# A graph network with routed experts on one core: four one-hot and message buffers in the value pass, the identity stored into the adjacency matrix beside the node MLP, and the last experts padded to 128 hidden units

## What is computed

```python
# layer 2, twice: softmax over the edges of a node, then its messages
msg = v[src] * alpha[:, :, None]
agg = jax.ops.segment_sum(msg, dst, num_segments=n).reshape(n, H * DV)
out = agg @ Wo
...
return jax.nn.relu(h @ w1 + b1) @ w2 + b2            # node MLP, 256 -> 1024 -> 256
# layer 3, three times: the neighbours' sum plus the node itself
pooled = jax.ops.segment_sum(msgs, row, num_segments=N_NODES) + h
hid = jax.nn.relu(_bn_train(pooled @ W1[l] + b1[l], g1[l], be1[l]))
# last experts: one of 32 per node, 256 -> 64 -> 256
h = jax.nn.relu(jnp.einsum('nd,ndh->nh', xf, w1t) + jnp.take(b1, idx, axis=0))
out = jnp.einsum('nh,nhd->nd', h, w2t) + jnp.take(b2, idx, axis=0)
```

## Time and profile before

| what | value |
|---|---|
| median of 3 runs | 6715.59 us (6714.32 to 6717.77) |
| the profiled execution: time, span of its instructions | 6709.0 us, 6707.0 us |
| mean granted clock of PE | 0.879 |
| PE busy | 5085.1 us, 76% |
| DVE, POOL, ACT busy | 2851.2, 2285.1, 1151.6 us |
| DMA | 949.50 MB, 142 GB/s on average |

### The profile page before, as it was taken

How to read it: one execution, slowest core, us unless ns; L and a number is a source line. 1 busy time by engine, 2 the same in 40 slices (tenths; PEclk the granted TensorE clock), 3 DMA queues, 4 the chain that set the end, 5 groups by cost and what they waited for, 6 DMA issues and landing times. The chain is left out here.

```text
span 6707.0 us, 87548 instructions
## 1 busy us (share of the span) xinstructions
PE 5085.1 (76%) x21976; PEld 3340.3 (50%) x21977; DVE 2851.2 (43%) x6134; ACT 1151.6 (17%) x2799; POOL 2285.1 (34%) x2415
## 2 busy tenths in 40 slices
PE   5657598979589795776496767496977997979857
PEld 3434475458435693443364433365876443434443
DVE  5575695041410424556685566685233102020242
ACT  2311251012100231111002111002322101010020
POOL 2786203704264050677230677230023000000014
PEclk9999999969789697889798888798978998989955
DMA  0000133427443262899572899571145332414134
GB/s 15 2 2 21 66 137 145 154 88 213 146 158 102 88 211 98 274 306 305 155 237 71 267 308 307 154 237 58 35 139 187 141 116 96 145 66 149 62 86 120
DMA packets 477264, 949.50 MB, mean 142 GB/s; under 512 B 111984, under 2 KB 285403, under 8 KB 474653
## 3 DMA queue, kind: packets, MB, share of 16 engines
q1 hardware_dynamic: 325308, 638.92, 28.2%
q0 software_dynamic: 114208, 281.05, 14.0%
q10 hardware_dynamic: 37568, 27.34, 1.4%
HBM read 732.28 MB, written 214.82 MB: 141 GB/s over the span
## 5 line engine op out<-in xcount | busy, mean ns | idle before, releaser
L1148 PE MATMUL banks<-ring,xn 128*128 128x512 f32 (+1 forms) x3500 | 1359.2, 551 | 144.4 <-DMA ring<-adjacency 144.4
L1148 PEld LDWEIGHTS banks<-ring,xn 128*128 128x128 f32 x3500 | 629.2, 192 | 862.5 <-issue 716.1
L991 POOL DMA_INDIRECT rows<-pairs,idxr x832 | 810.0, 974 | 239.3 <-issue 215.2
L1873 PE MATMUL banks<-agg,hotT 128*128 x1664 | 638.2, 488 | 235.3 <-issue 224.9
L1727 POOL IOTA found_i<- 128x25 int32 x4 | 0.6, 148 | 1808.1 <-ACTq L1723 1388.5
L381 POOL DMA_INDIRECT dst_table<-nodes_pay,nodes_row x392 | 378.8, 966 | 643.6 <-DVEq L1116 474.6
L1873 PEld LDWEIGHTS banks<-agg,hotT 128*128 128x128 f32 x1664 | 301.5, 223 | 522.6 <-issue 516.6
L381 POOL DMA_INDIRECT bin_table<-bins_pay,bins_row x392 | 457.9, 1168 | 270.2 <-DVE bins_row L767 119.1
L2126 PE MATMUL banks<-msg,hot 128*128 128x264 f32 x1664 | 429.0, 402 | 51.2 <-issue 24.9
L1846 DVE TENSOR_TENSOR prod<-banks,rows 128x512 f32<-128x512 f32 x416 | 267.9, 686 | 424.0 <-DMA rows<-pairs,idxr 311.6
L1056 PE MATMUL banks<-spans,lanes 128*128 128x256 f32 x1440 | 331.4, 387 | 119.5 <-DVE spans L1037 108.1
(11 more groups left out here) (350 smaller groups left out, 6798.6 us busy)
## 6 DMA issues: line engine op xcount, KB each, us to landing
ring<-adjacency SPq DMA_DIRECT2D x150, 1280.0 KB
spill<-rows SPq DMA_DIRECT2D x208, 512.0 KB
rows<-spill SPq DMA_DIRECT2D x208, 512.0 KB
w1r<-in_L_ffn_W SPq DMA_DIRECT2D x114, 512.0 KB
adjacency<-strips SPq DMA_DIRECT2D x13, 3200.0 KB
w1r<-in_L_ffn_w SPq DMA_DIRECT2D x65, 512.0 KB
rows<-home_rows SPq DMA_DIRECT2D x35, 640.0 KB
ring<-adjacency SPq DMA_DIRECT2D x25, 640.0 KB
```

What stands on the lines that cost most here:

```text
L991: nc.gpsimd.indirect_dma_start(rows[:, row, :], None, table, bass.IndirectOffsetOnAxis(ap=idxr[:, at + g:at + g + 1], axis=0))\
L1148: last = nc.tensor.matmul(K.ps[2 * (g % 2) + o][:, 0:wd], x[:, t * D + o * P:t * D + (o + 1) * P], ring[:, n % R, 0:wd // cols, q * SPAN_S ...
L1873: last = nc.tensor.matmul(K.ps[2 + 2 * (jj % 2) + g // 2][:, g % 2 * D:(g % 2 + 1) * D], hotT[:, jj % 2, g * P:(g + 1) * P], tile_of(q, t) ...
```

## The change

Three edits, independent of each other.

1. In `attention_values`, `hot` and `msg` have four buffers each, and DVE and POOL wait for PE's step i - 4. PE's program is the same but for the buffer that it reads.
2. `spmm` has no `own` any more. In `node_mlp`, SP loads the 25 diagonal squares (128x128) of the stored adjacency matrix, POOL adds the identity to them in one instruction, and SP writes them back and waits for that, so that the matrix that layer 3 reads holds the nodes themselves.
3. The last experts are padded with zeros to 128 hidden units: `b1T`, `w1r` and `hT` have 128 rows or columns, DVE clears `b1T` and `w1r` at the stage's start, and POOL clears the lower half of the second weights in the stage of the routing logits. All four expert stages have a new semaphore, `cleared`, for which SP waits ahead of its first fetch and ACT ahead of its bias loads; where the units are 512, DVE raises it at once.

```diff
@@ spmm
                                     ring[:, n % R, 0:wd // cols, q * SPAN_S:q * SPAN_S + cols],
-                                    start=(t == 0), stop=(t == NT - 1 and not own))
+                                    start=(t == 0), stop=(t == NT - 1))
                         last.then_inc(used, 1)
-                    if own:
-                        for q in range(wd // P):
-                            t = 4 * g + q
-                            for o in range(KD):
-                                last = nc.tensor.matmul(K.ps[2 * (g % 2) + o][:, q * P:(q + 1) * P],
-                                                        x[:, t * D + o * P:t * D + (o + 1) * P], K.ident[:, :],
-                                                        start=False, stop=(q == wd // P - 1))
-                        last.then_inc(summed, 1)
...
@@ class Second
+    def clear(self):
+        if self.hm < P:
+            self.nc.gpsimd.memset(self.second[self.hm:P, :], 0.0)
...
@@ routed_ffn
-        w1r = st.sb("w1r", [P, R, KD, hid])
+        w1r = st.sb("w1r", [P, R, KD, wide])
...
             def _(sp):
+                sp.wait_ge(cleared, 1)
...
-                                last = nc.tensor.matmul(K.ps[2 + jj % 2][0:hm, h * P:(h + 1) * P],
-                                                        w1r[:, jj, s, h * hm:(h + 1) * hm],
+                                last = nc.tensor.matmul(K.ps[2 + jj % 2][:, h * P:(h + 1) * P],
+                                                        w1r[:, jj, s, h * P:(h + 1) * P],
...
+                if hm < P:
+                    nc.vector.memset(b1T[:, :], 0.0)
+                    nc.vector.memset(w1r[:, :, :, :], 0.0).then_inc(cleared, 1)
+                else:
+                    dve.sem_inc(cleared, 1)
...
@@ attention_values
-        hot = st.sb("hot", [P, 2, GS, P])
-        msg = st.sb("msg", [P, 2, GS, W])
+        hot = st.sb("hot", [P, 4, GS, P])
+        msg = st.sb("msg", [P, 4, GS, W])
...
-                    wait_count(dve, summed, GS * (i - 1) + 1 if not isinstance(i, int) or i >= 2 else 0)
-                    one_hot(nc, edges, K, hot[:, j % 2, :, :], i)
+                    wait_count(dve, summed, GS * (i - 3) + 1 if not isinstance(i, int) or i >= 4 else 0)
+                    one_hot(nc, edges, K, hot[:, j, :, :], i)
...
@@ node_mlp
+    def diagonal(t):
+        at = t * SPAN_S + t % 2 * P
+        return K.adjacency[t // 2, :, at:at + P]
...
+                for t in range(NT):
+                    sp.dma_start(squares[:, t, :], diagonal(t)).then_inc(fetched, 16)
+                sp.wait_ge(raised, 1)
+                for t in range(NT):
+                    sp.dma_start(diagonal(t), squares[:, t, :]).then_inc(kept, 16)
+                sp.wait_ge(kept, 16 * NT)
+
+            @block.gpsimd
+            def _(pool):
+                pool.wait_ge(fetched, 16 * NT)
+                nc.gpsimd.tensor_tensor(squares[:, :, :], squares[:, :, :],
+                                        K.ident[:, :].unsqueeze(1).broadcast_to([P, NT, P]), ALU.add).then_inc(raised, 1)
```

More of the change, by code:

```diff
@@ L1096, in _, with spmm @@
                     sp.wait_ge(stored[h], 16 * ((NS + 1 - h) // 2))
-def spmm(nc, K, x, out, own=False, beside=None):
+def spmm(nc, K, x, out, beside=None):
     R, SLICE = 5, 5
@@ L1110, in spmm @@
         loaded = [st.sem(f"loaded{j}") for j in range(R)]
-        used, summed, kept = (st.sem(x) for x in ("used", "summed", "kept"))
+        used, kept = st.sem("used"), st.sem("kept")
         def width(g):
@@ L1164, in _ @@
                 for g in range(GROUPS):
-                    if own:
-                        act.wait_ge(summed, g + 1)
-                    else:
-                        act.wait_ge(used, (g + 1) * slices)
+                    act.wait_ge(used, (g + 1) * slices)
                     for o in range(KD):
@@ L1287, in dense @@
         with nc.Block() as block:
+            @block.gpsimd
+            def _(pool):
+                if ahead:
+                    ahead.clear()
             @block.sync
@@ L1518, in __init__ @@
         self.hm = min(P, self.hid)
-        self.second = st.sb("second", [self.hm, self.experts * (self.hid // self.hm) * D])
+        self.nc, self.second = st.nc, st.sb("second", [P, self.experts * (self.hid // self.hm) * D])
         self.w2 = w2
         self.whole = st.sem("whole")
+    def clear(self):
+        if self.hm < P:
+            self.nc.gpsimd.memset(self.second[self.hm:P, :], 0.0)
     def fetch(self, act):
-        act.dma_start(self.second[:, :].rearrange("p (n d) -> p n d", d=D),
+        act.dma_start(self.second[0:self.hm, :].rearrange("p (n d) -> p n d", d=D),
                       self.w2.rearrange("e (c p) d -> p (e c) d", p=self.hm)).then_inc(self.whole, 16)
@@ L1533, in routed_ffn @@
     nh = hid // hm
+    wide = nh * P
     n = r.chunks
@@ L1537, in routed_ffn @@
     with stage(nc) as st:
-        b1T = st.sb("b1T", [hm, experts * nh])
-        w1r = st.sb("w1r", [P, R, KD, hid])
+        b1T = st.sb("b1T", [P, experts * nh])
+        w1r = st.sb("w1r", [P, R, KD, wide])
         bias2 = st.sb("bias2", [P, experts * D])
@@ L1542, in routed_ffn @@
         xT = st.sb("xT", [P, 2, D])
-        hT = st.sb("hT", [hm, 2, nh * P])
+        hT = st.sb("hT", [P, 2, nh * P])
         yr = st.sb("yr", [P, R, D])
@@ L1547, in routed_ffn @@
         stored = [st.sem(f"stored{j}") for j in range(R)]
-        spread = st.sem("spread")
+        spread, cleared = st.sem("spread"), st.sem("cleared")
         biased, turned, copied, hidden, acted, summed, written = (
@@ L1621, in _ @@
             def _(act):
-                act.dma_start(b1T[:, :], b1.rearrange("e (c p) -> p (e c)", p=hm)).then_inc(biased, 16)
+                act.wait_ge(cleared, 1)
+                act.dma_start(b1T[0:hm, :], b1.rearrange("e (c p) -> p (e c)", p=hm)).then_inc(biased, 16)
                 act.dma_start(bias2[:, :], b2.rearrange("e d -> (e d)").partition_broadcast(P)).then_inc(spread, 16)
@@ L2106, in step @@
                 def step(i, j, k):
-                    wait_count(pool, summed, GS * (i - 1) + 1 if not isinstance(i, int) or i >= 2 else 0)
-                    nc.gpsimd.tensor_copy(msg[:, j % 2, :, D:W], weights[:, bass.ds(i * (GS * HEADS), GS * HEADS)]
+                    wait_count(pool, summed, GS * (i - 3) + 1 if not isinstance(i, int) or i >= 4 else 0)
+                    nc.gpsimd.tensor_copy(msg[:, j, :, D:W], weights[:, bass.ds(i * (GS * HEADS), GS * HEADS)]
                                           .rearrange("p (c h) -> p c h", h=HEADS)).then_inc(placed, 1)
@@ L2125, in step @@
                         pe.wait_ge(evacuated, v & 31)
-                        nc.tensor.matmul(K.banks[:, bass.ds((v % BANKS) * 512, W)], hot[:, j % 2, g, :], msg[:, j % 2, g, :],
+                        nc.tensor.matmul(K.banks[:, bass.ds((v % BANKS) * 512, W)], hot[:, j, g, :], msg[:, j, g, :],
                                          start=False, stop=True, skip_group_check=True).then_inc(summed, 1)
@@ L2158, in node_mlp @@
         hT = st.sb("hT", [P, 2, hid])
+        squares = st.sb("squares", [P, NT, P])
+        fetched, raised, kept = st.sem("fetched"), st.sem("raised"), st.sem("kept")
         loaded, staged, biased, turned, copied, hidden, acted, summed, added = (
@@ L2458, in layer3_gnn @@
         for l in range(layers):
-            spmm(nc, K, K.xn, K.agg, own=True)
+            spmm(nc, K, K.xn, K.agg)
             feature_layer(nc, K, K.agg, False, A["L3_gnn_W1"][l], A["L3_gnn_b1"][l], yT, S)
```

6 lines of the change are left out of this document (3 added, 3 removed).

## The result

| what | before | after |
|---|---|---|
| median of the runs | 6715.12 us, 4 runs (6714.32 to 6717.77) | 6588.71 us, 4 runs (6587.49 to 6590.15) |
| ratio | | 0.9817, interval 0.9805 to 0.9829 |
| the profiled execution: time, span | 6709.0, 6707.0 us | 6588.37, 6586.3 us |
| PE busy | 5085.1 us | 4944.6 us |

The account below looks back on a forecast made before the run. Bounds by stretch: PE-DVE hand-over in the value passes, PE in layer 3's products, PE with tile-shape changes in the last experts. Terms -66 - 34 - 13 + 1.5 = -111.5 from 6709.0 give 6597.5, plus 6.6: 6604 us, range 6580 to 6645.

Parts of the forecast that it names:

- a step of 1.87 us: Value passes: with four buffers the step falls from 2.20 to 1.87 us, 66 us less over two passes.
- near the upper end, because of the marks: Value passes: 1.87 us chosen between 1.78 and 1.92, because PE's four marks a step are not in its matmul rate.
- The 1.92 of the earlier trace: Upper bound of the value step, from the stage building the adjacency matrix: same PE program, 1.92 us a step, DVE 99% busy.
- some 60: Node MLP: the chain of loads, POOL's addition and stores lasts some 60 us at most, far inside the stage's 180.
- The 1 us at the start: Last experts' start: DVE's clearing of 1056 elements takes 0.9 us ahead of weight and bias loads, 1 us more.
- The 0.5 us for the semaphore: Three other expert stages: the new semaphore costs 0.1 to 0.2 us each, 0.5 us more.
- The offset to the median: Whole kernel: the median of the runs lies 6.6 us above the profiled execution, so 6597.5 becomes 6604 us.
- POOL's copy too late: Value passes: DVE, almost without gaps, keeps POOL's copy waiting; 6622 to 6670 us, chance 0.18.
- Padding brings nothing: Last experts: the 0.6 us between groups may come from PE reading the expert's number and stay; 6617 us, chance 0.17.
- Slower: Node MLP: the squares' chain of loads, add and stores outlasts the stage; 6744 us if it lasted 320, chance 0.03.
- the ring: Value passes: PE's and DVE's work and two hand-overs, 4.44 us, over two buffers 2.22 a step, over four 1.11.

Follow-up runs that it names:

- value_only: The kernel before with only the changed `attention_values` (four buffers of one-hots and messages): 7657.24 us, ratio 0.9893.
- own_left_out: The kernel before without layer 3's 50 matmuls against the identity and with nothing in their place: 7693.42 us, ratio 0.9932.
- half_before: The kernel before with the scatters of every second chunk of the last experts left out: 7780.31 us, ratio 0.9977, last experts 183.0 us.
- unroll12: The changed kernel with twelve steps instead of four in the value pass's loop body: 7678.84 us, ratio 0.9856.
- half_after: The changed kernel with the scatters of every second chunk of the last experts left out: 7651.24 us, ratio 0.9819, last experts 165.9 us.
- unroll12_again: The changed kernel with twelve steps in the value pass's loop body, run once more: passes 198.7 and 196.0 us.

## Why the prediction was right, and where its size was off

**Edit 1: the step fell as argued, its term was 7 us too small.** The prediction took a step of 1.87 us between bounds of 1.78 and 1.92 and said 66; measured was 1.84 and 73.1 (80 on the other chips). The bound of 1.78 was the step that runs, three times in four; "near the upper end, because of the marks" was the failed choice. The marks are read in every step and cost nothing in a step of 1.78. What lengthens a step by 0.28 comes once in a body of four and is gone with a body of twelve. The 1.92 of the earlier trace rows was a bound set by DVE and said nothing of PE. The other chips' passes are 6.6 us shorter in sum: the passes of the first chip have one wait of 2.5 us for POOL and 45 steps longer than 1.9 us, those of value_only no such wait and 32.

**Edit 2: right in all its terms.** 34.5 for 34 us in the products; cost in the node MLP +0.4 for 0 (0 to 3), with a chain of 35 us for "some 60" at most; the start delayed by 0.3 (PE's first record 9.27 us after SP's first load, 8.95 before). own_left_out shows, by its stages, that nothing of the saving is lost.

**Edit 3: right on the first chip, and only there.** 14.5 for 12 us: POOL's period in steady state is 2.57 where I had 2.55, PE takes no part, and PE's own chunk at the low clock is 2.13 us where I had 2.19. The term holds only while each chunk's sum is there when POOL comes to scatter it, a condition that the prediction did not name. On the other chips the padding gave 2 to 3 us in one trace and nothing in the next. That the limit before was PE at 2.80, and not POOL, was argued; half_before shows that 2.80 is PE's own pace. The 1 us at the start was about right: DVE's clearing of `w1r` takes 0.91 us, and PE's first record of the second product is 21.3 us after the stage's start where it was 19.8 (its very first records, transposes, came sooner, 3.9 us for 5.6). The 0.5 us for the semaphore in the three other expert stages does not show: they differ by +0.2, -0.3 and 0.0. POOL's clearing of the second weights takes 6.92 us under the routing logits, where the stage did not grow.

**The offset to the median** is 6 of the 15 us by which the forecast was high. I took the profiled execution of before to be 6.6 us below the median because it was, and added the 6.6 after; the changed kernel's profiled execution stands 0.3 below its own median. The rest is edit 1's 7 and edit 3's 2.5, less 1 or so in the other stages. The prediction's own range of 6583 to 6616 does not come out of its terms; edit 1's bounds and 4 us of edit 2 give 6586 to 6618. The measured 6588.71 lies in both.

**The rivals.** POOL's copy too late: real, 2.5 us once, at the first pass's start, and nowhere in the steady state. Its price was set for a copy locked out in every step. Steady copies last 0.755 us with DVE 97% busy, and so they do in unroll12 with DVE 100% busy. The difference seen in the rows is that in the steady state both instructions start together, while at the start DVE has buffers free and waits for nothing. That alone is not the cause: every pass with four buffers starts so, and the copy was through in 0.81 or 0.93 us in eight of twelve. What decides stays open. The Trainium skill (SBUF — State Buffer, "SBUF: two separate sides") has the shared port taken for a whole instruction by whoever is first. The steady 0.755 agrees with a copy that gets in at an instruction's end; the 7.77 us does not, it outlasts eight of DVE's instructions. The measurement decides: the copy can be passed over again and again.

Padding brings nothing: not so on the first chip; PE's own chunk became shorter, 2.13 for 2.81 us at the same clock, and half_before and half_after agree, with 372 and 410 records in the same time. Slower: nothing of it, the chain takes 35 of 195 us.

## What to carry to other kernels

When two engines wait for each other's buffers in turn, add the four parts of the ring (both works, both hand-overs), divide by the number of buffers, and compare with each engine alone; once buffers have made the ring harmless, look at each engine's own step, and next at a cost that comes once in a loop body. Read a stage that seems to be at PE's pace for its clock and its tile shapes before believing it: 64 of 128 rows or columns filled made PE "busy" for all of the stage at a clock of 0.50. And where a saving leaves the engine that issues indirect transfers as the bound, measure it in a second comparison: here it was 14.5 us in one and 0 to 3 in the others.

## What the hardware showed that I had not expected

- **A POOL copy of 32 elements took 7.77 us** beside a row of two-input instructions on DVE, against 0.755 in the steady state and 0.35 for two with DVE idle. The same copy takes 0.93 us in one pass of unroll12_again and 7.89 in the other. The copy ahead of it, the fourth of a pass, took 4.9 us in all twelve passes with four buffers, beside DVE's clearing of the banks; nothing waited for it, and its cause is open.
- **The same program took 15 to 16% longer on three chips than in the first comparison**, and nearly all of it lies in seven stages with POOL's indirect DMAs: 472 us instead of 278 for the product beside the table, with PE at 91 records in 200 us instead of 468, though POOL's instruction and its gap (0.966, 0.30 us) were the same, and the DMAs' packets moved no later behind them.
- **PE's clock went up when its tiles were filled, though it was busy for less of the time.** In the last experts the granted clock is 0.50 with half-width tiles and PE "busy" for 130 of 130 us, 0.84 with full tiles and PE busy for 94.5. With the first product full and the second one at 64 rows it is 0.50.
- **A loop turn can show on PE**: 0.28 us once in a body of four steps, and next to nothing with a body of twelve.
